# A decoder layer with a mixture of experts: plain float32 second layers for three early tiles, and another order of work around them

## The reference

```
x = x + linear_attention(layernorm(x))       # phi(Q), phi(K), 16 heads of 16
x = x + cross(layernorm(x), ctx, ctx)        # l2-normed projections, one sum over keys
x = x + moe(layernorm(x))                    # top 2 of 8 experts
# one expert: h = gelu(xn @ W1 + b1);  y = h @ W2 + b2;  added with the gate as its weight
# W1: 256 x 1024, W2: 1024 x 256, all float32
```

## Time and profile before

| | |
|---|---|
| median of 3 runs | 455.47 us (453.4 to 457.32) |
| the profiled execution | 459.77 us |
| its span, first to last instruction | 457.7 us |
| mean granted TensorE clock | 0.968 |
| PE busy | 412.2 us (90%) |
| DVE busy | 355.9 us (78%) |
| ACT busy | 322.5 us (70%) |
| POOL busy | 242.9 us (53%) |
| moved by transfers | 79.60 MB, mean 174 GB/s |

### The profile page before, as it was taken

One profiled execution on the slowest core, in us unless ns is written; L12 is line 12 of the kernel. 1 busy time (PEld: TensorE's weight loads), 2 busy tenths in 40 slices (PEclk: granted clock), 3 DMA queues, 4 the chain that ended last, 5 costly groups with the idle time before them and its releaser, 6 DMA issues.

```text
span 457.7 us, 8784 instructions
## 1 busy us (share of the span) xinstructions
PE 412.2 (90%) x2929; PEld 384.9 (84%) x2929; DVE 355.9 (78%) x839; ACT 322.5 (70%) x635; POOL 242.9 (53%) x350
## 2 busy tenths in 40 slices
PE   0689999999999988698799899999999999999980
PEld 0578888889898866688799899999999999999980
DVE  1735666877878878889589977997999899979960
ACT  2465576666756567692987968988988899888720
POOL 3234456466655556488684655452555646445441
PEclk9999999999999989799799999999999999999996
DMA  8900020202110253751718989699798979896721
GB/s 270 339 4 26 24 69 25 69 26 69 46 51 24 84 183 129 267 185 49 254 50 252 300 244 320 200 313 321 214 333 291 313 230 375 264 319 189 190 34 11
DMA packets 32464, 79.60 MB, mean 174 GB/s; under 512 B 4674, under 2 KB 23746, under 8 KB 26532
## 3 DMA queue, kind: packets, MB, share of 16 engines
q1 hardware_dynamic: 23456, 67.94, 42.5%
q0 software_dynamic: 7488, 10.39, 11.7%
q10 hardware_dynamic: 1476, 0.72, 0.6%
HBM read 69.40 MB, written 9.63 MB: 173 GB/s over the span
## 4 chain that ended last, share of the span: by engine, by line
PE 68%; POOL 12%; DVE 10%; issue 5%; ACT 2%; DMA 2%; POOLq 0%; ACTq 0%; DVEq 0%
PE bank L401 55%; PE bank L408 4%; PE bank L674 2%; DVE ohB L1342 1%; PE bank L804 1%; POOL rb L1875 1%; PE bank L633 1%; PE bank L640 1%; PE bank L694 1%; POOL rs L1836 1%; PE bank L615 1%; POOL cT_l L1994 1%; DMA xg<-xn_rows,idxg 1%; DVE st L1278 1%; DMA y_<-yb,idxs 1%
## 5 line engine op out<-in xcount | busy, mean ns | idle before, releaser
L2033 POOL DMA_INDIRECT y_<-yb,idxs x29 | 55.8, 1923 | 75.8 <-DMA y_<-yb,idxs 42.9
L401 PE MATMUL bank<-w2h,hh 128*128 128x256 f32 x312 | 88.9, 285 | 0.0
L401 PE MATMUL bank<-w2l,hh 128*128 128x256 f32 x312 | 87.6, 281 | 0.0
L401 PE MATMUL bank<-w2h,hl 128*128 128x256 f32 x312 | 87.5, 281 | 0.0
L401 PE MATMUL bank<-xh,w1h 128*128 128x256 f32 x256 | 76.0, 297 | 1.3 <-DVE w1l L1394 0.8
L401 PE MATMUL bank<-xh,w1l 128*128 128x256 f32 x256 | 73.9, 289 | 0.0
L401 PE MATMUL bank<-xl,w1h 128*128 128x256 f32 x256 | 73.9, 289 | 0.0
L1137 ACT ACTIVATE hf<-bank,bs 128x256 f32<-128x256 f32 x128 | 51.9, 480 | 10.6 <-PE bank L401 9.5
L401 PEld LDWEIGHTS bank<-w2h,hh 128*128 128x128 f32 x312 | 59.1, 189 | 0.0
L401 PEld LDWEIGHTS bank<-w2l,hh 128*128 128x128 f32 x312 | 59.1, 189 | 0.0
L401 PEld LDWEIGHTS bank<-w2h,hl 128*128 128x128 f32 x312 | 59.0, 189 | 0.0
(11 more groups left out here) (252 smaller groups left out, 1042.0 us busy)
## 6 DMA issues: line engine op xcount, KB each, us to landing
w1r<-ff_ SPq DMA_DIRECT2D x23, 1024.0 KB, 6.4
w2r<-ff_ SPq DMA_DIRECT2D x23, 1024.0 KB, 6.9
b1r<-b_ SPq DMA_DIRECT2D x7, 512.0 KB, 7.3
bs<-ff_ SPq DMA_DIRECT2D x23, 132.0 KB, 5.9
xn_rows<-xn SPq DMA_DIRECT2D x8, 264.0 KB, 3.4
xin<-x_ SPq DMA_DIRECT2D x8, 256.0 KB, 6.7
cT<-ctxT_ SPq DMA_DIRECT2D x8, 256.0 KB, 3.5
cin<-ctx_ SPq DMA_DIRECT2D x8, 256.0 KB, 3.5
```

The lines of the kernel that those rows point to most:

```text
L401: r = e.matmul(o, a_(t), b_(t), start=first and m == 0, stop=m == n - 1)
L2033: e.indirect_dma_start(out=out[:, :], out_offset=bass.IndirectOffsetOnAxis(ap=at, axis=0), in_=yb[t % 2][:, i, :], in_offset=None, compute ...
```

## The change

1. `layer2(t, i)` for t < `NP` = 3 multiplies `hidden(t, j)` with `w2r` as plain float32: 8 products for a half in place of 24. For these tiles there is no `w2_high`, `w2_low`, `h_high` and `h_low`. The counts of semaphores that these pieces raise start at tile 3 (`split(t)`).
2. The GELU of these tiles writes to `hp0` and `hp1`, which lie over `hh0` and `hh1`, two buffers in turn, in place of the one `hf`. `layer2` waits for the weights' transfer and the eighth GELU.
3. `load_w2(t)` for t = 2 to 4 waits for the products of tile t-2 (`m_l2`) rather than for the subtraction from its weights.
4. From the end of the batch loop to tile 4, the lists of all five engines are in another order. All pieces but the splitting ones above are still there.

```diff
 NH = 7
 KIND = "FFFFF" + "FFHFFHFHFFHFHFFHFH"
 NT = len(KIND)
+
+NP = 3
 NX = NF + NH
 TAB = [(NE + NF if k == "H" else 0) + KIND[:t].count(k) for t, k in enumerate(KIND)]
...
 lies_over(73984, 73792)
 hf = sb("hf", [P, 8, 256])
+
+with ExitStack() as plain:
+    hp0 = sb("hp0", [P, 8, 256], fp32, plain)
 hh0 = sb("hh0", [P, 8, 256], f32r)
 xh0 = sb("xh0", [P, 2, 256], f32r)
 xl0 = sb("xl0", [P, 2, 256], f32r)
 ya = sb("ya", [P, 2, D])
 hl0 = sb("hl0", [P, 8, 256], f32r)
+with ExitStack() as plain:
+    hp1 = sb("hp1", [P, 8, 256], fp32, plain)
 hh1 = sb("hh1", [P, 8, 256], f32r)
 xg3 = sb("xg3", [P, 2, DG])
 xg4 = sb("xg4", [P, 2, DG])
...
 b1r = sb("b1r", [P, F])
 w1r, w1h, w1l = [w1r0, w1r1], [w1h0, w1h1], [w1l0, w1l1]
 w2r, w2h, w2l = [w2r0, w2r1], [w2h0, w2h1], [w2l0, w2l1]
+hp = [hp0, hp1]
 xh, xl, hh, hl, yb = [xh0, xh1], [xl0, xl1], [hh0, hh1], [hl0, hl1], [yb0, yb1]
...
 def gathered(t):
     return 16 * sum(ROWS[n] for n in range(t % RING, t + 1, RING))
+
+def split(t):
+    return 2 * (t - NP)
+
 def halves_of(t):
     return 2 * KIND[:t].count("H")
...
 def bank7(b):
     return 2 if b == NB - 1 else 4
+
+
+def hidden(t, j):
+    return hp[t % 2][:, j, :] if t < NP else hf[:, j, :]
 def high_on_act(t):
...
         if t == 1:
             e.wait_ge(p_c1, 2 * NB)
             e.wait_ge(g_cTl, NB)
-        if t >= 2:
-            e.wait_ge(m_w2l, 2 * (t - 1))
+        if 2 <= t < NP + 2:
+            e.wait_ge(m_l2, BEFORE[t - 1])
+        if t >= NP + 2:
+            e.wait_ge(m_w2l, split(t - 1))
         e.dma_start(w2r[k][:, :], expert(t, 2048, 4096)).then_inc(d_w2[k], 16)
     def write_residual(b):
...
             load_w2(0)
         if s >= 2:
             write_residual(s - 2)
+    write_rows(NB - 3)
     load_w1(1)
     load_b(1)
     load_w2(1)
-    write_rows(NB - 3)
     load_w1(2)
     load_b(2)
     write_residual(NB - 2)
     load_w1(3)
     load_w2(2)
+    load_b(3)
     write_rows(NB - 2)
+    load_w1(4)
     write_residual(NB - 1)
-    load_w1(4)
     load_w2(3)
-    load_b(3)
+    load_b(4)
     write_rows(NB - 1)
+    load_w1(5)
     load_w2(4)
-    load_w1(5)
-    load_b(4)
     for t in range(5, NT):
         if t + 1 < NT:
             load_w1(t + 1)
...
             if q < 2:
                 e.wait_ge(m_hb, halves_of(t - 1) + q + 1)
             else:
-                e.wait_ge(m_hl, 2 * (t - 1) + q - 1)
+                e.wait_ge(m_hl, split(t - 1) + q - 1)
         for m in range(2):
             c = slice((2 * q + m) * 128, (2 * q + m + 1) * 128)
             last = three(e, banks[bank1(t, q)][:, m * 256:(m + 1) * 256],
...
     def layer2(t, i):
         k = t % 2
-        if i == 0:
-            e.wait_ge(m_w2l, 2 * t + 2)
-            e.wait_ge(m_hl, 2 * t + 2)
+        if i == 0 and t < NP:
+            e.wait_ge(d_w2[k], 16 * (t // 2 + 1))
+            e.wait_ge(m_hf, 8 * t + 8)
+        if i == 0 and t >= NP:
+            e.wait_ge(m_w2l, split(t) + 2)
+            e.wait_ge(m_hl, split(t) + 2)
         if t >= 1 and i < ROWS[t - 1]:
             e.wait_ge(m_ya, BEFORE[t - 1] + i + 1)
         if t >= 2 and i >= ROWS[t - 1]:
             e.wait_ge(m_ya, BEFORE[t - 1])
         c = slice(i * 128, (i + 1) * 128)
+        if t < NP:
+            for j in range(8):
+                last = e.matmul(banks[5 + i][:, 0:D], hidden(t, j)[:, c],
+                                w2r[k][:, :].rearrange("p (j n) -> p j n", j=8)[:, j, :], start=j == 0, stop=j == 7)
+            last.then_inc(m_l2, 1)
+            return
         three(e, banks[5 + i][:, 0:D], lambda j: hh[k][:, j, c], lambda j: hl[k][:, j, c],
               lambda j: w2h[k][:, :].rearrange("p (j n) -> p j n", j=8)[:, j, :],
               lambda j: w2l[k][:, :].rearrange("p (j n) -> p j n", j=8)[:, j, :], 8, True).then_inc(m_l2, 1)
     attended(NB - 1)
+    count(NB - 3)
     xpose(0)
     projected(NB - 1)
-    count(NB - 3)
+    layer1(0, 0)
+    xpose_n(NB - 2)
+    layer1(0, 1)
     invert(NB - 3)
-    xpose_n(NB - 2)
-    layer1(0, 0)
-    layer1(0, 1)
+    layer1(0, 2)
     xpose_2(NB - 1)
+    layer1(0, 3)
     gate_logits(NB - 2)
-    layer1(0, 2)
-    layer1(0, 3)
+    second(NB - 1)
+    layer2(0, 0)
     xpose(1)
-    second(NB - 1)
     rank(NB - 2)
+    layer2(0, 1)
     xpose(2)
     layer1(1, 0)
+    invert(NB - 2)
     layer1(1, 1)
-    invert(NB - 2)
-    layer2(0, 0)
+    xpose_n(NB - 1)
     layer1(1, 2)
-    layer2(0, 1)
-    xpose_n(NB - 1)
     layer1(1, 3)
     layer1(2, 0)
     gate_logits(NB - 1)
     layer1(2, 1)
+    rank(NB - 1)
+    layer2(1, 0)
+    invert(NB - 1)
+    layer2(1, 1)
+    inverse()
+    layer1(2, 2)
     xpose(3)
-    rank(NB - 1)
-    layer1(2, 2)
-    layer2(1, 0)
     layer1(2, 3)
-    layer2(1, 1)
-    invert(NB - 1)
+    xpose(4)
     layer1(3, 0)
-    inverse()
-    xpose(4)
+    layer2(2, 0)
     layer1(3, 1)
+    layer2(2, 1)
+    select()
     layer1(3, 2)
     layer1(3, 3)
-    layer2(2, 0)
-    layer2(2, 1)
-    select()
-    for q in range(4):
-        layer1(4, q)
+    layer1(4, 0)
+    layer1(4, 1)
+    layer1(4, 2)
+    layer2(3, 0)
+    layer1(4, 3)
     xpose(5)
-    layer2(3, 0)
     layer2(3, 1)
     for t in range(5, NT):
         if KIND[t] == "H":
...
     def w2_high(t, c):
         k = t % 2
         e.wait_ge(d_w2[k], 16 * (t // 2 + 1))
-        if t == 1:
-            e.wait_ge(p_at, 2 * NB)
-        if t >= 2:
-            e.wait_ge(m_l2, BEFORE[t - 1])
+        e.wait_ge(m_l2, BEFORE[t - 1])
         s = slice(c * 1024, c * 1024 + 1024)
         e.activation(w2h[k][:, s], w2r[k][:, s], ACT.Copy).then_inc(m_w2h, 1)
...
         e.wait_ge(m_l1, 4 * t + q + 1)
         if q == 0:
             e.wait_ge(d_bs[t % 3], 16 * (t // 3 + 1))
-        if t == 0 and q == 0:
+        if t == 1 and q == 0:
+            e.wait_ge(p_s7, 2 * NB)
+        if t == 2 and q == 0:
+            e.wait_ge(m_l2, BEFORE[1])
+        if t == NP and q == 0:
             e.wait_ge(g_xc, NB - 1)
-        if q % 2 == 0 and t >= 1:
-            e.wait_ge(m_hl, 2 * (t - 1) + q // 2 + 1)
+        if q % 2 == 0 and t > NP:
+            e.wait_ge(m_hl, split(t - 1) + q // 2 + 1)
         if q == 0 and t >= 1 and KIND[t - 1] == "H":
             e.wait_ge(m_ht, halves_of(t))
         for m in range(2):
             j = 2 * q + m
-            e.activation(hf[:, j, :], banks[bank1(t, q)][:, m * 256:(m + 1) * 256], ACT.Gelu_apprx_tanh,
+            e.activation(hidden(t, j), banks[bank1(t, q)][:, m * 256:(m + 1) * 256], ACT.Gelu_apprx_tanh,
                          bias=bs_[t % 3][:, j:j + 1]).then_inc(m_hf, 1)
     def h_high(t, c):
         e.wait_ge(m_hf, 8 * t + 4 * c + 4)
-        if t >= 2 and c == 0:
+        if c == 0:
             e.wait_ge(m_l2, BEFORE[t - 1])
         s = slice(4 * c, 4 * c + 4)
         e.activation(hh[t % 2][:, s, :], hf[:, s, :], ACT.Copy).then_inc(m_hh, 1)
...
     e.activation(gelu_at[:, :], eps[:, 2:3], ACT.Gelu_apprx_tanh)
-    w2_high(0, 0)
     attended(NB - 1)
-    w2_high(0, 1)
     x_affine(0)
     x_high(0)
     out_high(NB - 1)
-    w1_high(1, 0)
-    w1_high(1, 1)
-    residual(NB - 2)
     xn_affine(NB - 2)
-    w2_high(1, 0)
     gelu(0, 0)
-    w2_high(1, 1)
-    x2T_high(NB - 1)
     gelu(0, 1)
     gelu(0, 2)
-    h_high(0, 0)
+    x2T_high(NB - 1)
+    residual(NB - 2)
     gelu(0, 3)
+    w1_high(1, 0)
+    squares_q(NB - 1, 0)
+    squares_q(NB - 1, 1)
+    w1_high(1, 1)
+    w1_high(2, 0)
+    w1_high(2, 1)
     x_affine(1)
-    squares_q(NB - 1, 0)
     x_high(1)
-    h_high(0, 1)
-    squares_q(NB - 1, 1)
+    weigh(0, 0)
     x_affine(2)
-    w1_high(2, 0)
     x_high(2)
-    w1_high(2, 1)
     gelu(1, 0)
+    weigh(0, 1)
     gelu(1, 1)
-    h_high(1, 0)
+    xn_affine(NB - 1)
     gelu(1, 2)
-    residual(NB - 1)
-    w2_high(2, 0)
-    xn_affine(NB - 1)
-    w2_high(2, 1)
+    w1_high(3, 0)
     gelu(1, 3)
-    weigh(0, 0)
-    h_high(1, 1)
-    w1_high(3, 0)
+    w1_high(3, 1)
     gelu(2, 0)
-    w1_high(3, 1)
-    weigh(0, 1)
+    gelu(2, 1)
+    weigh(1, 0)
+    weigh(1, 1)
+    gelu(2, 2)
     x_affine(3)
-    gelu(2, 1)
     x_high(3)
-    gelu(2, 2)
-    h_high(2, 0)
     w1_high(4, 0)
     gelu(2, 3)
     w1_high(4, 1)
-    h_high(2, 1)
-    weigh(1, 0)
+    residual(NB - 1)
+    x_affine(4)
     gelu(3, 0)
-    weigh(1, 1)
+    x_high(4)
     w2_high(3, 0)
+    w2_high(3, 1)
     gelu(3, 1)
-    w2_high(3, 1)
     h_high(3, 0)
     gelu(3, 2)
-    x_affine(4)
     gelu(3, 3)
-    x_high(4)
     h_high(3, 1)
-    w2_high(4, 0)
-    w2_high(4, 1)
-    gelu(4, 0)
     weigh(2, 0)
-    gelu(4, 1)
     w1_high(5, 0)
-    gelu(4, 2)
     weigh(2, 1)
     w1_high(5, 1)
+    gelu(4, 0)
+    w2_high(4, 0)
+    gelu(4, 1)
+    w2_high(4, 1)
+    gelu(4, 2)
+    h_high(4, 0)
     x_affine(5)
     gelu(4, 3)
-    h_high(4, 0)
     h_high(4, 1)
     for t in range(5, NT):
         if KIND[t] == "H":
...
     def w2_low(t, c):
         k = t % 2
-        e.wait_ge(m_w2h, 2 * t + c + 1)
+        e.wait_ge(m_w2h, split(t) + c + 1)
```

(94 more changed lines are left out.)

## The result

The changed kernel takes 449.23 us (median of 4 runs, 447.23 to 450.2) beside 455.26 us of the kernel before (4 runs). The ratio, run against run, is 0.9845 with a 95% interval of 0.9802 to 0.9887: 7.1 us faster, between 5.1 and 9.0. The forecast was 445.6 us in a range of 441.0 to 452.5, and faster by over 1%. The side is right and the range holds the time; the gain of 9.9 us was forecast some 3 us too large.

A forecast was written before the change was run, and what follows sets the result against it. From batch loop's end to tile 3's last product, hand-ordered ACT and DVE lists keep TensorE waiting. 176.3 start + 67.2 work + 3.6 plain products + 4.3 idle = 251.4 against 261.3 us: gain 9.9, forecast 445.6 us, range 441.0 to 452.5.

The forecast's parts named there:

- The plain product: Second layers of tiles 0 to 2: 48 plain products at 0.432 us replace 144 split ones, 3.6 us more TensorE work.
- Rival C: Six plain half layers run at the 1.2 GHz level, 20.7 us more, 466.3 us; chance 0.05.
- Step 2: Tile 1's first weights load some 7 us later, still covered; second(7) waits 0.4 us for x2T_low.
- Step 3: rank(6) issued behind layer2(0,0), DVE pieces queued behind it; TensorE stands 1.1 us at invert(6).
- Step 5: xpose(3) and xpose(4) share a bank; xl(3) comes late, 0.7 us wait before layer1(3,0).
- Step 6: POOL's residual_factors(7), just covered, leads to a write with load_w2(3) behind it; 1.5 us wait before layer2(3,0).
- Step 7: Tile 5's gather, behind rows() on POOL, lands before xpose(5): no wait.
- Rival A: Late residual_factors(7) on POOL holds back load_w2(3), tile 3 slips whole: 451 to 454.6 us; chance 0.20.
- the low clock: TensorE at 1.2 GHz in the stage: forecast none left, 6.2 us lost to it before.
- Rival B: One low-clock stretch in the stage's new waits, 3.4 us more, 449.0 us; chance 0.10.
- what the stage gains, the whole gains: Behind the stage TensorE never waits and the program is unchanged, so the stage's 9.9 us gain carries through.
- Rival D: Weight transfers set the pace behind 261 us, so the stage's gain is waited away: 455.5 us; chance 0.05.

The follow-up runs named there:

- e4: The changed kernel with each of the 48 plain products made twice; ratio to the kernel before 1.0217, 17.0 us over the changed kernel.
- e3: The changed kernel with load_w2(3) and load_b(4) issued ahead of write_residual(7) on SP; ratio to the kernel before 0.9788.
- e1: The kernel before with plain second layers for tiles 0 to 2, its old lists otherwise kept; ratio to the kernel before 1.0004.
- e12: e1 with own_rank(5), route_b(5) and x_split(0) moved early on DVE, layer1(0,0) ahead of invert(5) on TensorE; ratio to the kernel before 0.9989.
- e9: The changed kernel measured again unchanged, with more rounds and a second profile; ratio to the kernel before 0.9842.
- e8: The changed kernel with e3's swap, e5's two moves, and gather(6) ahead of scatter(2,0) on POOL; 445.35 us, ratio to the kernel before 0.9739.
- e7: The changed kernel with four plain tiles in place of three (tile 3 plain too); ratio to the kernel before 0.9822.
- e10: e8 with a fourth plain tile (tile 3's splitting left out); ratio to the kernel before 0.9797, 2.6 us over e8.
- e2: The changed kernel's new lists with every product split as before, splitting pieces of tiles 0 to 2 put back; ratio to the kernel before 1.003.
- e5: The changed kernel with rank(6) ahead of layer2(0,0) on TensorE, x_affine(1) and x_high(1) ahead of both w1_high(2) on ACT; ratio to the kernel before 0.9872.
- e11: e8 with xpose(3) ahead of layer1(2,2) on TensorE, x_affine(3) and x_high(3) ahead of gelu(2,2) on ACT; ratio to the kernel before 0.9778.
- e6: The changed kernel with two plain tiles in place of three (tile 2 split again); ratio to the kernel before 0.989.

## Why the prediction was right, and where it was off

**The sum, term by term**, in the first profile. Work at full clock: 72.70 - 3.4/2 = 71.0 us, forecast 67.2 + 3.6 = 70.8. Waits: 77.63 - 72.70 = 4.9 us, forecast 4.3. Low clock: 1.7 us, forecast none. Together 77.6 against 75.1 us (251.4 - 176.3). Behind the stage 0.7 us were lost, forecast none. 2.5 + 0.7 = 3.2 us is the gap between a gain of 9.9 and the 6.6 of the profiles. Put as a balance, the stage gained 6.7 us of waits and 4.5 us of low clock and paid 3.8 us of work.

**The plain product** at 0.432 us was right to 0.002 us, and e4 shows that its price is paid in full. Rival C, the low level under plain products, fell: none of the six half layers ran at 0.50 in either profile.

**The waits** were placed well, though not their sum term by term. Start of the stage: 0.34 us for `kvc`, forecast 0.6 with `xn`. Step 2: none, forecast 0.4. Step 3: 0.87 us at `invert(6)`, forecast 1.1, and 0.81 for `xl(1)`, for which the sum had no term; I had let DVE's list set it, but it was ACT, where the two `w1_high(2)` ahead of `x_affine(1)` waited 3.0 us for a load issued at 187.2. Step 5: 0.78 us, forecast 0.7. Step 6: 1.64 and 1.92 us, forecast 1.5, by the chain I named; e3 shows it by taking it away. Step 7: 0.43 us for `xpose(5)` and 0.50 for `xpose(6)`, forecast none. Both are gone in e3, where the swap brings `rows()` and the gathers earlier.

Rival A did not happen: `residual_factors(7)` ended at 225.0 and ACT came to `residual(7)` at 225.6, so POOL was not late, and its instruction `rb` took 0.22 us this time:

```profile
224.77 0.22 POOL L1881 TENSOR_SCALAR rb<-rb 128x2 f32<-128x2 f32 x1
```

That is less luck than it seemed. In the kernel before, in e1 and in e12 the slow POOL instruction lasted 4.30, 3.17 and 3.17 us and each time ended within 0.02 us of the end of a run of DVE's two-input operations. Here no such run was under way: DVE made small pieces until `w1_low(4,0)` at 225.57. So what has to be laid out for POOL is DVE's list beside it, and not a spread of sizes. One step of the chances doesn't follow either: A as priced gives 451.3 us or more, at best 0.9% faster than before, and yet half of it was counted as faster by over 1%.

**The term that was mis-sized is the low clock**: forecast at nothing in the stage, measured at 1.7 us in the first profile and 3.4 in e9. The argument was that a stretch at 0.50 follows a wait of 2.1 us or more, since 1.8 us had brought none. It fell behind 1.92 us (e9), and the kernel before already spoke against it, in its first 40 us:

```profile
18.85 0.80 PE L567 MATMUL bank<-ab_r,one_r 128*128 128x512 f32 x1 [2.06 <-DVE ab_r L1411]
...
30.16 0.66 PE L408 MATMUL bank<-cs,xln 128*128 128x128 f32 x4 [1.01 <-DVE wkv L1503]
...
32.20:35.60 3.40, 3.40 (x17) 3.22 (x16) 0.15 (x1) 1.79 (x5) 0.00 (x0) 0.50 0.02 5
```

A wait of 2.06 us was followed by full clock, and one of 1.01 us, 2 us later, by a stretch at 0.50.

Nor did the sum allow for a stretch with no wait of size in front of it. In three profiles of kernels with the new lists (the first, e9 and e8) one falls within `projected`, at 175.3 to 177.5, at a place without a wait of 0.5 us. It isn't the stretch of the batch loop come later, since e9 and e8 have one in the batch loop as well; for e8:

```profile
163.79:167.19 3.40, 3.40 (x11) 2.78 (x10) 3.33 (x12) 2.70 (x4) 1.93 (x2) 0.50 0.33 97
...
177.45:180.86 3.41, 3.41 (x11) 2.70 (x10) 2.62 (x9) 2.07 (x5) 2.85 (x8) 0.50 0.23 79
```

What brings it there stays open. Rival B, which I gave 0.10, had a low stretch in the new waits: that is what e9 shows in front of `layer2(3,0)`, but not the first profile. Its size was 1.7 us and not 3.4, since a stretch of 3.4 us costs half its length.

**The reasoning behind "what the stage gains, the whole gains"** held for this change, with 0.7 us lost. Rival D fell, as loads of weights kept up. The reasoning is not general, though: e7 and e10 wait 1.67 and 1.18 us for a weights' buffer behind the stage, and e3's profile loses 1.4 us with its last scatters.

**The split of the cause** I had only in part. I called the splitting room, and the orders the decisive steps. e1, e2 and e12 show that none of these three parts pays by itself. That the forecast came out well owes to all the lists having been laid out together: the same kind of step counted by itself, with the wait it removes, promised 4.5 to 7 us for e12 and gave none.

## What to carry to other kernels

Where lists written by hand bound a stage, don't add up the waits that an edit removes: lay out all engines to the end of the stage, since a removed wait comes back at the next late piece (e12, e5), and only the piece on the last chain pays (e3: one swapped line, 2.0 us less waiting). Look on the transfer queue first for a load that stands behind a write of something late, and ask of each buffer what frees it after the change (e7, e10). And compare profiles by stages from an event to an event: of the 9.3 us between these two spans, 2.7 came from code that was the same. Take the low clock out before you compare: without that, e11's stage looks 1.2 us shorter than e8's and is 0.5 us longer.

## What the runs showed of the hardware that was not expected

- Inside the kernel the low stretches of TensorE (granted 0.50) lasted 3.4 or 6.8 us, and the length of the wait in front did not decide whether one came. The same wait of 2.07 to 2.12 us near 163 was followed by one within 1.5 us in 11 of 14 profiles and by none in three (the changed kernel's first, e10, e11). Waits of 1.92 to 1.95 us were followed by one (e9, twice in e2), those of 1.57 to 1.82 us by none (before, changed kernel, e2, e6, e7), but one of 1.01 us was (before, near 30 us).
- A plain float32 product of 128x128 by 128x256 shows as two records of 0.215 us each, 0.43 us, against 3 x 0.119 = 0.36 us for the three split ones: it costs only a fifth more on TensorE, and neither rounding nor subtraction elsewhere. Made twice, 48 of them added 20.3 us of busy time.
- Instructions of POOL on 128x2 elements that took 0.22 and 0.82 us in the changed kernel (the pieces of `rb`) lasted 4.30, 3.17 and 3.17 us (before, e1, e12) while DVE ran operations with two inputs without a break, and ended at 216.83, 211.60 and 208.86 us, where DVE's runs ended at 216.81, 211.59 and 208.84.
